# Attention passes of a four-layer graph network: the spreading product moved behind the turned differences, gathers bound to their buffer alone

## What is computed

```python
xp = (x @ W).reshape(n, HEADS, C)
a_src = einsum('nhc,hc->nh', xp, att_src); a_dst = einsum('nhc,hc->nh', xp, att_dst)
alpha = leaky_relu(a_src[src] + a_dst[dst] + a_edge, 0.2)      # a_edge in layer 2 only
ea = exp(alpha - segment_max(alpha, dst)[dst])
attn = ea / segment_sum(ea, dst)[dst]
out = segment_sum(xp[src] * attn[:, :, None], dst)
```

## Time and profile before

| what | us |
|---|---|
| median of three runs | 5967.39 |
| profiled execution | 5958.41 |
| its span, first to last instruction | 5956.3 |
| layer 1's pass (L869 gathers) | 1806 to 2906 |
| layer 2's attention pass | 3074 to 4340 |
| last layer's attention pass | 4537 to 5830 |

### The profile page before, as it was taken

The page is one execution under the profiler, slowest core; times in us unless marked ns, Lnnn a source line. Parts: engine busy times, 40 slices in busy tenths (PEclk is TensorE's granted clock), DMA queues, the critical chain, the costliest instruction groups (busy, mean ns, idle before and its releaser), DMA issues. The chain is left out here.

```text
span 5956.3 us, 90473 instructions
## 1 busy us (share of the span) xinstructions
PE 4291.7 (72%) x22227; PEld 3328.4 (56%) x22228; DVE 3976.5 (67%) x8362; ACT 3118.9 (52%) x8998; POOL 3418.9 (57%) x3592
## 2 busy tenths in 40 slices
PE   4799999999775666666656666666665666666666
PEld 2577777777564555555545555555524555555552
DVE  4688888888653333333467777777775777777777
ACT  3799999999544444444444344343343434333332
POOL 2466666666106777777426666666603666666660
PEclk8899999999888888888777777777787777777777
DMA  7333333333214554554334444444304444444442
GB/s 255 96 94 93 93 93 94 93 93 93 67 36 136 135 136 133 135 135 133 111 101 126 129 130 124 129 129 124 111 6 121 123 122 123 125 121 126 120 110 90
DMA packets 677753, 676.59 MB, mean 114 GB/s; under 512 B 457142, under 2 KB 546135, under 8 KB 675851
## 3 DMA queue, kind: packets, MB, share of 16 engines
q0 software_dynamic: 173552, 491.76, 29.0%
q1 hardware_dynamic: 363791, 153.85, 10.1%
q10 hardware_dynamic: 140316, 29.88, 2.4%
HBM read 616.96 MB, written 57.70 MB: 113 GB/s over the span
## 5 line engine op out<-in xcount | busy, mean ns | idle before, releaser
L1852 POOL DMA_INDIRECT g3rows<-sender_rows,g3idx x880 | 840.1, 955 | 653.4 <-issue 254.8
L869 POOL DMA_INDIRECT g1rows<-rows,g1idx x880 | 831.7, 945 | 548.9 <-DMA g1idx<-src_of 281.2
L1103 POOL DMA_INDIRECT c0rows<-rows,c0idx x880 | 861.3, 979 | 484.4 <-issue 345.0
L1852 POOL DMA_INDIRECT g2rows<-sender_rows,g2idx x880 | 839.9, 954 | 515.0 <-issue 244.8
L1132 ACT ACTIVATE c0z<-c0rows,c0sh 128x128 f32<-128x128 f32 x2640 | 792.2, 388 | 0.0
L990 DVE TENSOR_TENSOR acc<-acc,g1psA 128x258 f32 x660 | 279.8, 424 | 720.7 <-PE g1psA L895 569.5
L898 PE MATMUL g1psA<-g1rows,g1sel 128*128 128x129 f32 x2640 | 472.8, 347 | 358.4 <-DMA g1rows<-rows,g1idx 318.6
L1884 PE MATMUL g3psA<-g3rows,g3sel 128*128 128x136 f32 x2640 | 468.9, 342 | 348.2 <-DVE g3rows L2078 268.5
L1884 PE MATMUL g2psA<-g2rows,g2sel 128*128 128x132 f32 x2640 | 452.4, 335 | 349.6 <-DVE g2rows L2078 266.7
L898 PEld LDWEIGHTS g1psA<-g1rows,g1sel 128*128 128x128 f32 x2640 | 453.5, 258 | 401.5 <-issue 347.1
L1884 PEld LDWEIGHTS g3psA<-g3rows,g3sel 128*128 128x128 f32 x2640 | 430.2, 244 | 401.0 <-issue 293.2
(11 more groups left out here) (439 smaller groups left out, 8938.3 us busy)
## 6 DMA issues: line engine op xcount, KB each, us to landing
g2bc<-dst_rows SPq DMA_DIRECT2D x55, 512.0 KB
g3bc<-dst_rows SPq DMA_DIRECT2D x55, 512.0 KB, 3.7
g1f<-in_edge_attr SPq DMA_DIRECT2D x103, 256.0 KB, 3.4
c0rows<-rows,c0idx POOLq DMA_INDIRECT x880, 2.8
g1rows<-rows,g1idx POOLq DMA_INDIRECT x880
g2rows<-sender_rows,g2idx POOLq DMA_INDIRECT x880
g3rows<-sender_rows,g3idx POOLq DMA_INDIRECT x880
rbf_steps<-prep_extra POOLq DMA_DIRECT2D x7, 1024.0 KB, 8.9
```

The source lines that it names most:

```text
L869: g.indirect_dma_start(rows[b][:, u, 0:D], None, k.table, bass.IndirectOffsetOnAxis(ap=idx[b][:, u:u + 1], axis=0)).then_inc(r_sem[b], 16)
L1103: g.indirect_dma_start(rows[b][:, m, place(n), :], None, k.table, bass.IndirectOffsetOnAxis(ap=idx[b][:, 4 * m + n:4 * m + n + 1], axis=0) ...
L1852: g.indirect_dma_start(rows[b][:, u, 0:TW], None, k.sender_rows, bass.IndirectOffsetOnAxis(ap=idx[b][:, u:u + 1], axis=0)).then_inc(gas[b] ...
```

## The change

In both attention passes:

- TensorE reads the tile numbers of spread(t + 1) at the head of body(t), ahead of quarter 0 of the sums, and the 16 products of spread(t + 1) come last, behind factors(t) and back(t).
- The end of the products is told by a semaphore of its own, `sp`. VectorE's transpose_hot and score wait for it where they waited for `dt`.
- `dt` no longer counts spread(0), so every user of it counts one less; the quarters all read their count with the same offset of 2.
- GpSimd waits once ahead of a set: for its numbers and for `dt` at t - 1, which is back(t - 2), in front of which the sums of round t - 3 are done. The waits before gathers 5, 7 and 9 are gone, and of four increments of `go` one is left.

```diff
--- before.py
+++ after.py
@@ -1757,7 +1757,7 @@
 
     names = ["ix0", "ix1", "ix2", "ln0", "ln1", "ln2", "hd0", "hd1", "hd2", "ae0", "ae1", "ae2", "bc",
              "init", "oh", "z", "zt", "loc", "tb", "tr", "lev", "arg", "cc", "cp", "cs", "al", "rs", "d", "dt", "w",
-             "msg", "sel", "acc", "c", "v", "mx", "go"]
+             "msg", "sel", "acc", "c", "v", "mx", "go", "sp"]
     es, s = scope(nc, [tag + n for n in names], [(tag + f"ga{b}", k.gathered.pop()) for b in range(3)])
     with es:
         S = {n: s[tag + n] for n in names + ["ga0", "ga1", "ga2"]}
@@ -1806,7 +1806,7 @@
         psA = pt("psA", [P, 2, 3, 512])
         block = es.enter_context(nc.Block())
         ix, lns, hds, aes, gas = ([S[n + str(b)] for b in range(3)] for n in ("ix", "ln", "hd", "ae", "ga"))
-        quarter = [(S["zt"], 2), (S["tb"], 2), (S["cc"], 2), (S["dt"], 3)]
+        quarter = [S["zt"], S["tb"], S["cc"], S["dt"]]
         turned, others, ends_, starts = slice(0, P), slice(P, 2 * P), slice(2 * P, 3 * P), slice(0, P)
         factor, brought = slice(3 * P, 3 * P + H), slice(3 * P + H, 3 * P + H + 2)
         full = 16 * U
@@ -1815,8 +1815,7 @@
 
         def summed(eng, t, q):
 
-            sem, more = quarter[q]
-            reach(eng, sem, t + more)
+            reach(eng, quarter[q], t + 2)
 
         @block.sync
         def _(sp):
@@ -1835,7 +1834,7 @@
                     sp.dma_start(ae[b][:, :], k.edge_steps[ds(t * U, U), :].rearrange("u (h e) -> h u e", h=H)
                                  ).then_inc(aes[b], 16)
                 if later(i):
-                    sp.wait_ge(S["dt"], t - 1)
+                    sp.wait_ge(S["dt"], t - 2)
                 sp.dma_start(hd[b][:, :], k.heads[ds(t, 1), :]).then_inc(hds[b], 16)
 
             triples(sp, NB, load)
@@ -1844,11 +1843,9 @@
         def _(g):
             def gather(t, b, i):
                 g.wait_ge(ix[b], i * 16 + 16)
-                behind = {0: S["dt"], 5: S["zt"], 7: S["tb"], 9: S["cc"]}
+                reach(g, S["dt"], t - 1)
+                g.sem_inc(S["go"], 1)
                 for u in range(U):
-                    if u in behind:
-                        reach(g, behind[u], t)
-                        g.sem_inc(S["go"], 1)
                     g.indirect_dma_start(rows[b][:, u, 0:TW], None, k.sender_rows,
                                          bass.IndirectOffsetOnAxis(ap=idx[b][:, u:u + 1], axis=0)
                                          ).then_inc(gas[b], 16)
@@ -1857,16 +1854,18 @@
 
         @block.tensor
         def _(pe):
-            def spread(t, b, i):
-                _, at = nc.values_load_multi_w_load_instructions(
+            def tiles_of(t):
+                return nc.values_load_multi_w_load_instructions(
                     k.node_of[0:1, ds(t * K, U)], engines=[PE], min_val=0, max_val=NT - 1,
-                    skip_runtime_bounds_check_because="made in prepare() from counts of at most NT - 1")
+                    skip_runtime_bounds_check_because="made in prepare() from counts of at most NT - 1")[1]
+
+            def spread(t, at):
                 pe.wait_ge(S["oh"], t + 1)
                 reach(pe, S["z"], t)
                 for u in range(U):
                     ins = nc.tensor.matmul(psE[:, u * 3 * H:(u + 1) * 3 * H], oneT[:, u * P:(u + 1) * P],
                                            wide(k.recv[:, ds(at[u], 1), :]), start=True, stop=True)
-                return ins
+                ins.then_inc(S["sp"], 1)
 
             def sums(t, b, q):
                 half = q // 2
@@ -1921,6 +1920,9 @@
             def body(t, b, i):
                 before = (b - 1) % 3
                 first = isinstance(t, int) and t == 0
+                last_one = isinstance(t, int) and t == NB - 1
+                if not last_one:
+                    at = tiles_of(t + 1)
                 if not first:
                     sums(t - 1, before, 0)
                 turn(t)
@@ -1932,16 +1934,16 @@
                 columns(t, b, i)
                 if not first:
                     sums(t - 1, before, 3)
-                if not (isinstance(t, int) and t == NB - 1):
-                    spread(t + 1, (b + 1) % 3, i + (b + 1) // 3)
                 factors(t, b, i)
                 back(t)
+                if not last_one:
+                    spread(t + 1, at)
 
             pe.wait_ge(S["init"], 6)
-            spread(0, 0, 0).then_inc(S["dt"], 1)
+            spread(0, tiles_of(0))
             triples(pe, NB, body)
             for q in range(4):
-                sums(NB - 1, (NB - 1) % 3, q).then_inc(quarter[q][0], 1)
+                sums(NB - 1, (NB - 1) % 3, q).then_inc(quarter[q], 1)
 
         @block.scalar
         def _(a):
@@ -1971,12 +1973,12 @@
                 nc.scalar.activation(inc[0:1, 1, :].rearrange("o (h u) -> o h u", h=H), ob[0:1, :, 1:K], ACT.Copy
                                      ).then_inc(S["cp"], 1)
                 a.wait_ge(S["arg"], t + 1)
-                reach(a, S["dt"], t + 1)
+                reach(a, S["dt"], t)
                 nc.scalar.activation(al[:, :], arg[:, :], ACT.Exp).then_inc(S["al"], 1)
                 a.wait_ge(S["cc"], t + 1)
                 reach(a, S["d"], t)
                 nc.scalar.activation(cin[:, :], psT[0:HU, brought], ACT.Copy).then_inc(S["cs"], 1)
-                a.wait_ge(S["dt"], t + 2)
+                a.wait_ge(S["dt"], t + 1)
                 by = rows[b][:, :, 0:TW].rearrange("p u (h c) -> p h u c", c=HW)[:, :, :, CH]
                 if own:
                     nc.scalar.activation(rows[b][:, :, TW:RW].rearrange("p u h -> p h u"),
@@ -1997,13 +1999,13 @@
 
             def transpose_hot(t, b, i):
                 v.wait_ge(S["bc"], t * 16 + 16)
-                reach(v, S["dt"], t)
+                reach(v, S["sp"], t)
                 nc.vector.tensor_scalar(oneT[:, :], bc[:, :], k.lane[:, 0:1], None, ALU.is_equal
                                         ).then_inc(S["oh"], 1)
 
             def score(t, b, i):
                 v.wait_ge(gas[b], i * full + full)
-                v.wait_ge(S["dt"], t + 1)
+                v.wait_ge(S["sp"], t + 1)
                 reach(v, S["zt"], t)
                 a_src = rows[b][:, :, 0:TW].rearrange("p u (h c) -> p h u c", c=HW)[:, :, :, CH]
                 part = psE[:, 0:U * 3 * H].rearrange("p (u q h) -> p q h u", q=3, h=H)
@@ -2058,7 +2060,7 @@
 
             def differ(t, b, i):
                 v.wait_ge(S["cs"], t + 1)
-                reach(v, S["dt"], t + 1)
+                reach(v, S["dt"], t)
                 nc.vector.scalar_tensor_tensor(out=m1[:, :], in0=ln[b][:, pref], scalar=cin[:, 0:1], in1=loc[:, :],
                                                op0=ALU.add, op1=ALU.max).then_inc(S["v"], 1)
                 v.wait_ge(S["v"], t * 9 + 9)
```

## The result

The kernel after took 5690.2 us (median of 4 runs, 5684.35 to 5693.46) against 5967.01 us for the kernel before beside it: a ratio of 0.9537, 95% interval 0.952 to 0.9553. That is 276.8 us less; 282 were predicted (5686, range 5666 to 5765). The profiled execution took 5684.35 us, its span is 5682.6.

A forecast was written before the change was run, and what follows sets the result against it. A chain with VectorE waiting for L1919 bounds the attention passes; rounds of 22.42 and 23.00 us fall to the gathers' 20.1, saving 125 + 157 = 282 us: 5676 profiled, 5686 us with the median 9.0 above; range 5666 to 5765.

The forecast's parts named there:

- The hole: VectorE's fourth quarter of additions waits for TensorE's transpose L1919, 235.6 and 238.5 us in the two attention passes.
- some 190 us: Part of the 474 us of VectorE's waits for L1919 not to be had, as the gathers take over as bound.
- Rival B: Attention passes: the VectorE-TensorE loop stays the bound, 20.6 and 20.9 us a round, 5756 us; chance 0.22.
- C: Gathers without stops crowd each other and the small loads, 23.7 us a round, 6074 us; chance 0.05.
- D: Moved load and products delay TensorE's first sums by all they save at L1919, 5967 us; chance 0.03.
- the 1.3 us excess: TensorE, slow rounds: products, load and dispatch after L1919 outlast the wait for weighted rows by 1.3 us, delaying the turn.
- a cover of 4.89: TensorE's 4.89 us wait for weighted rows, in which the moved products and register load were to hide.
- The ring: VectorE-TensorE loop from one start of the fourth additions to the next: means 19.6 us in layer 3, 19.9 in layer 2.
- the edit of the gathers: GpSimd without the stops inside a set: the gathers' own pitch then holds it, 20.1 us a round.
- the comparison: VectorE's bf16 comparison, one a round, stretches GpSimd's gathers by 0.1 us a round, between 0 and 0.38.
- The 0.38 end: VectorE's comparison holds up a gather fully every round: 20.4 us a round, 33 us less gain.

The follow-up runs named there:

- twelve_before: The kernel before with 12 of the 16 gathers of each round, the other rows left at zero: 5962.42 us, ratio 0.9993.
- twelve_after: The kernel after with 12 of the 16 gathers of each round, the other rows left at zero: 5519.97 us, ratio 0.9248.
- load_old_place: The kernel after with the register load back behind the fourth quarter of sums, ahead of the factors; only the products come last: 5707.65 us, ratio 0.9576.
- load_late: The kernel after with the register load directly ahead of the 16 products, behind `back`: 5686.79 us, ratio 0.9538.
- order_only: The kernel after with the old stops ahead of gathers 5, 7 and 9 put back: 5687.64 us, ratio 0.9541.
- compare_ahead_again: The kernel after with VectorE's bf16 comparison between the score's second and third additions, no longer behind the score: 5727.1 us, ratio 0.9597.
- after_again: The kernel after, unchanged, on another chip where the kernel before takes 6601.07 us: 7319.64 us, ratio 1.1089.
- compare_one_port: The kernel after with VectorE's comparison as a tensor_tensor against a bf16 copy of the lane number, replacing tensor_scalar: 5806.65 us, ratio 0.9734.

## Why the prediction was right, and where it was not

**Right.** The hole was the bound, it went as described (2.10 us from `df` to the additions; 19.6 and 15.8 us left of 235.6 and 238.5), and a large part of its 474 us was not to be had, because the gathers took over at 20.17 and 20.14 us against 20.1. `twelve_before` and `twelve_after` show both halves of that. The part was put at some 190 us; from the rings of `twelve_after` it is 54 x (1.71 + 1.38) = 167 us, since 19.6 + 15.8 = 35 us of the hole remain as waits. Rival B (ring the bound) held in none of the rounds; the nearest to it is the last layer of `load_old_place`. C and D did not happen; C's point, crowded gathers, is refuted by a pitch of 1.260 us at 138 GB/s.

**Wrong step 1: the 1.3 us excess.** The prediction laid products (2.07 us), load (3.80 us) and dispatch end to end, 6.2 us, into a cover of 4.89. The excess was none. The products took 0.69 us. With that instead the sum is 4.8 us, inside the cover, and on the timeline the load is over 0.5 us before it would matter. The 2.07 us of the earlier trace rows belong to the place behind a load: `load_late` puts the products back there and they take 2.09 us. That elsewhere their instructions are readied by the sequencer while TensorE waits is the reading that fits; no run shows it directly. `load_late` shows a second slip: a load may begin before `back` is done, so load and products need not fit end to end into the cover. The ring is 18.46 and 18.76 us, not 19.6 and 19.9. As the gathers were the bound, nothing of this reached the time.

**Wrong step 2: what the edit of the gathers is for.** The prediction asked only "Taken away, what holds GpSimd?", and not what the stops still cost beside the shorter ring. Measured, they cost nothing once the counts they wait for come early (`order_only` 0.9541 against 0.9537).

**Term of the sum: the comparison.** 0.1 us of stretch a round was taken, between 0 and 0.38. Measured are 0.11 in layer 2 and 0.10 in the last layer. The 0.38 end was a real one, only for another phase: `compare_ahead_again` has 0.43 and 0.34. That 0.1 and not 0.38 came out was luck of the phase: the argument for it, the median of all gathers, can't see a stretch that hits one gather in sixteen.

**Chances.** The 0.05 for slower were given to crowded gathers. The chip of `after_again` shows a slowdown by something on no list of mine.

## What to carry to other kernels

When a chain is cut, first work out from the trace where the next bound stands, here 16 gathers at an undisturbed pass's pitch: it, not the size of the hole, gives the gain, and it says which of the other edits are worth making. Read an instruction's duration in the place where it stands: behind a register load 16 products took 2.07 us, ahead of a wait, with no load before them, they took 0.69. And when an engine's fixed pitch is the bound, the phase of whatever disturbs it is a parameter of the kernel: try the places, don't reason them. Last, a gain measured on some chips may not hold on another: here 4.6% less on those, 10.9% more on one.

## What the hardware showed that I had not expected

- A gather has two sensitive places. Starting 0.1 to 0.3 us ahead of the bf16 comparison it ends 0.12 us behind that; starting 0.1 to 0.4 us into it, it ends 0.82 us behind it, 1.2 to 1.47 us long in all. Of those that started 0.02 to 0.09 us into it most kept their 0.95 us. What a gather does in those places no run shows.
- A tensor_tensor with both inputs and its output in SBUF stops a gather as well, but only in one of the two places (`compare_one_port`): gathers that started 0.02 to 0.5 us ahead of it kept their 0.95 us, those that started 0.04 us or more into it ended 0.82 us behind its end, up to 3.06 us long.
- The load of 16 registers takes 3.80 us in three rounds of four and 1.1 us in the fourth, wherever it stands (28 of 110 are short before, after, in `load_late` and in `load_old_place`). In `load_old_place`, but for the first and last rounds, the way from `df` to the end of `back` is 3.9 to 4.6 us in three rounds and 1.9 in each fourth. Why is open.
- Chips can differ by 11% in the kernel before and by 29% in the kernel after (7319.64/5690.2), with the same durations of single instructions on VectorE, ScalarE and GpSimd; only TensorE's are longer, at a lower granted clock. What is late there is above all one handover, from TensorE's L1897 to ScalarE's L1967, by some 11 us a round. The cause is open.
